# SyncE waits for the last scatter, and GpSimd has a second DRAIN

## The chip, the cores and the metric

The kernel runs on one NeuronCore of a Trainium2 chip (trn2). The metric is the time of one execution on the device in microseconds, lower is better. All data are float32, a few tables are bfloat16. The core has five engines with an instruction queue each: TensorE (PE in the profile, its weight loads PEld), VectorE (DVE), ScalarE (ACT), GpSimd (POOL) and SyncE (SP). A q behind a name (POOLq) is the engine's queue or sequencer. DMAs are issued from SP, ACT and POOL.

## The reference: what is computed

`x` has 4 x 256 tokens of 256 channels. Four residual steps follow each other:

```python
x = x + tanh(g_xattn[0]) * graph_attention(ctx_512, layernorm(x), ...)   # two layers
x = x + tanh(g_ffn[0])   * gated_ffn(layernorm(x), ...)                   # 704 wide
x = x + tanh(g_xattn[1]) * top_k_attention(ctx_512, layernorm(x), Wq, Wk, gamma)
x = x + tanh(g_ffn[1])   * mixture(layernorm(x), gate_w, w1, w2, w3)
```

The change touches the end of the last step, the mixture of experts. Eight experts of width 512 stand ready, and each token uses the two with the highest scores:

```python
h = silu(einsum('th,efh->etf', x, w1)) * einsum('th,efh->etf', x, w3)
y = einsum('etf,ehf->eth', h, w2)
coef = (one_hot(sel, 8) * mult[..., None]).sum(axis=1)
out = einsum('te,eth->th', coef, y)
```

## The kernel before, in words

Each engine has its own program, and semaphores order them. The normalised tokens are stored as rows in DRAM (`xn3_dram`), and `x` after the attention is stored in the output (`out`) by SP. The mixture then works in blocks of 128 tokens that share an expert. For each block POOL gathers the block's rows from `xn3_dram` with an indirect DMA, TensorE turns them and multiplies them by the expert's weights, ScalarE and VectorE do the activation and the product, TensorE multiplies by `w2`, ScalarE scales the result by the token's coefficient (`scale_y`), and POOL adds the rows to `out` with an indirect DMA that accumulates (a scatter).

There are 16 blocks with a place of their own (`STATIC` = 16). Blocks 0 to 7 are of the first half of the tokens, blocks 8 to 15 of the second. `AT` = 10: between block 9 and block 10 stands a loop over pairs of overflow blocks, whose number is read from data; on these inputs it runs once. An overflow block gathers with `fetch_over` and scatters in two halves of 64 rows (`scatter_over`).

Scatters are in strict order. `scatter(j)` waits on the semaphore `scattered` until every scatter before it has landed, since two blocks can add to the same row. After the last one, the program before waits once more at line 769 for all of them, and at line 771 for the gathers of the overflow blocks, which were issued long before. Then the program ends.

The end of the program is not written in the kernel: the instructions that close it are put down under line 69. Each engine has a branch, a DRAIN (an instruction that is finished when the engine has finished what is behind it), and then a meeting of all five engines by EVENT_SEMAPHORE instructions, which POOL gathers and releases. At the program's start (line 2262) stands such a meeting too, with a DRAIN on each engine.

POOL's order of work is a list, `POOL_ORDER`, that is written out by hand; the loop at lines 735 to 749 goes through it. Around the place of the change it reads: scatter 5, the gathers of overflow blocks 0 and 1 (line 715), scatter 6, gathers 10 and 11, scatter 7, gathers 12 and 13, scatter 8, the gathers of overflow blocks 2 and 3, scatter 9, gathers 14 and 15. Scatters of blocks are line 707, gathers of blocks line 687, and the gathers of the graph step (`gather_rows`) line 666.

SP's program issues loads and stores, and ends with waits for its stores (lines 582 and 583). It has nothing else to do from there on.

The semaphores `row_picked` tell VectorE that a gather of line 666 has landed; before there were eight of them, one for each tile.

Of the kernel before, what the change touches and what calls it, by code (L numbers as in the profile page):

```python
# [43 lines left out]
HT = T // 2  # L44
# [18 lines left out]
def build(nc, x_in, ctx2_in, g_xattn, g_ffn, gamma, w0_in, w0T_in, b0_in, w1_in, w1T_in, a_in, b1_in,  # L63
# [5 lines left out]
    with ctx:  # L69
# [3 lines left out]
        def sem(name):  # L73
            return ctx.enter_context(nc.semaphore(name))
# [256 lines left out]
        feat_exp = sem("feat_exp")  # L331
        token_ready = sem("token_ready")
        feat_stored = [sem(f"feat_stored{b}") for b in range(B)]
        row_picked = [sem(f"row_picked{t}") for t in range(T)]
        x_squared = sem("x_squared")
        norms_ready = sem("norms_ready")
        lead_ready = sem("lead_ready")
# [54 lines left out]
        y_done = sem("y_done")  # L392
        y_scaled = sem("y_scaled")
        scattered = sem("scattered")

        CONSTS = 23
        HIDDEN_BANK = FEAT_BANK = (6, 4)
# [67 lines left out]
                      ("gather", 0), ("gather", 1), ("gather", 2), ("gather", 3), ("attn_stats", 2), ("attn_stats", 3),  # L465
                      ("gather", 4), ("gather", 5), ("gather", 6), ("gather", 7), ("moe_stats", 2), ("moe_stats", 3),
                      ("scatter", 0), ("scatter", 1), ("scatter", 2), ("scatter", 3), ("gather", 8), ("scatter", 4), ("gather", 9),
                      ("scatter", 5), ("gather_over", 0), ("gather_over", 1), ("scatter", 6), ("gather", 10), ("gather", 11), ("scatter", 7),
                      ("gather", 12), ("gather", 13), ("scatter", 8), ("gather_over", 2), ("gather_over", 3), ("scatter", 9),
                      ("gather", 14), ("gather", 15)]  # L470

# [43 lines left out]
        @block.sync  # L515
        def _(sp):
            xv = x_in.rearrange("(t p) c -> p t c", p=P)
            sp.dma_start(ctx2[:, 0:N], ctx2_in[:, 0:N]).then_inc(ctx_loaded[0], 16)
            sp.dma_start(w0x[:, 0:H * FO], w0_in).then_inc(w0_loaded, 16)
            sp.dma_start(w1x[:, :, 0:H * FO], w1_in.rearrange("(k p) n -> p k n", p=P)).then_inc(w1_loaded, 16)  # L520
            sp.dma_start(x[:, 0:HT, :], xv[:, 0:HT, :]).then_inc(x_loaded[0], 16)
            sp.dma_start(ctx2[:, N:2 * N], ctx2_in[:, N:2 * N]).then_inc(ctx_loaded[1], 16)
            sp.dma_start(gates[:, 0:2], rows(g_xattn)).then_inc(gates_loaded, 16)
            sp.dma_start(gates[:, 2:4], rows(g_ffn)).then_inc(gates_loaded, 16)
            sp.dma_start(gates[:, 4:5], rows(gamma)).then_inc(gates_loaded, 16)
            sp.dma_start(x[:, HT:T, :], xv[:, HT:T, :]).then_inc(x_loaded[1], 16)
            def load_up(w, src):
                sp.dma_start(w[:, :, :], src.rearrange("(k p) n -> p k n", p=P)).then_inc(ffn_loaded, 16)

            load_up(gw, gw_in)  # L530
            def load_expert(e):
                load_weights(e, ((e1, e1_in), (e3, e3_in), (e2, e2_in)))

            def load_weights(e, pieces):
                for w, src in pieces:
                    sp.dma_start(w[:, e * 1024:(e + 1) * 1024], src[e]).then_inc(experts_loaded[e], 16)

            def load_down():
                sp.dma_start(dw[:, 0:FULL, :], dw_in[0:FULL * P, :].rearrange("(k p) n -> p k n", p=P))\
                  .then_inc(down_loaded, 16)  # L540
                sp.dma_start(dw[P - TAIL:P, FULL, :], dw_in[FULL * P:INTER, :]).then_inc(down_loaded, 16)
                sp.dma_start(dsr[:, :], rows(ds_in)).then_inc(down_loaded, 16)

            def load_general():
                sp.dma_start(b1[:, :], rows(b1_in)).then_inc(b1_loaded, 16)
                for q in range(2):
                    sp.dma_start(ctxT.rearrange("d (c q n) -> d c q n", c=2, q=2)[:, :, q, :],
                                 ctx2_in[q * D:(q + 1) * D, :].rearrange("d (c n) -> d c n", c=2)).then_inc(whole_ctx_loaded, 16)

            for b in range(B):  # L550
                if b == 2:
                    load_up(uw, uw_in)
                    for v, src in ((gs, gs_in), (us, us_in)):
                        sp.dma_start(v[:, :], src).then_inc(ffn_loaded, 16)
                    load_general()
                sp.wait_ge(token_ready, b + 1)
                sp.dma_start(f_dram[b].rearrange("(t p) c -> p t c", p=P),
                             feat[:, 2 * b:2 * b + 2, :]).then_inc(feat_stored[b], 16)
            load_down()
            sp.dma_start(rg[:, :, :], rg_in.rearrange("(k p) n -> p k n", p=P)).then_inc(router_loaded, 16)  # L560
            sp.wait_ge(graph_over, T)
            for e in (0, 1, 2, 3, 4, 7):
                load_expert(e)
            for p, (t, n) in enumerate(PARTS):
                if p == 2:

                    sp.wait_ge(ffn_u_done, 2 * FULL)
                    sp.wait_ge(ffn_g_done, 2 * IT)
                    for e in (5, 6):
                        load_weights(e, ((e1, e1_in), (e3, e3_in)))  # L570
                    sp.wait_ge(down_done, len(PARTS))
                    for e in (5, 6):
                        load_weights(e, ((e2, e2_in),))

                sp.wait_ge(x3_ready, p + 1)
                sp.dma_start(out.rearrange("(t p) c -> p t c", p=P)[:, t:t + n, :],
                             xr[:, t:t + n, :]).then_inc(out_stored[p], 16)
                sp.wait_ge(xn_ready, XT["turn_moe", p] + 1)
                sp.dma_start(xn3_dram.rearrange("(t p) c -> p t c", p=P)[:, t:t + n, :],
                             xn[:, t % HT:t % HT + n, :]).then_inc(rows_stored[p], 16)  # L580
            for p in range(len(PARTS)):
                sp.wait_ge(out_stored[p], 16)
                sp.wait_ge(rows_stored[p], 16)


        @block.gpsimd
        def _(pool):
# [72 lines left out]
            def gather_rows(b):  # L660

                pool.wait_ge(index_ready, b // 2 + 1)
                pool.wait_ge(feat_stored[b], 16)
                for t in range(2 * b, 2 * b + 2):
                    pool.sem_inc(pool_passed)
                    pool.indirect_dma_start(  # L666
                        out=picked[:, t, :], out_offset=None, in_=f_dram[b],
                        in_offset=bass.IndirectOffsetOnAxis(ap=gix[:, t:t + 1], axis=0),
                        bounds_check=last_node, oob_is_err=False).then_inc(row_picked[t], 16)

            def wait_rows(h):

# [19 lines left out]
            def scatter(j):  # L692

                h, at = place(j)
                if j == 0:
                    pool.wait_ge(out_stored[0], 16)
                    pool.wait_ge(out_stored[1], 16)
                if j == E:
                    pool.wait_ge(out_stored[2], 16)
                    pool.wait_ge(out_stored[3], 16)  # L700
                pool.wait_ge(y_scaled, j + 1)
                if j >= AT:
                    pool.wait_ge(scattered, pairs * 64 + 16 * j)
                elif j:
                    pool.wait_ge(scattered, 16 * j)
                pool.sem_inc(pool_passed)
                pool.indirect_dma_start(  # L707
                    out=out, out_offset=bass.IndirectOffsetOnAxis(ap=ids[h][:, at:at + 1], axis=0),
                    in_=yv[kept_in(j)], in_offset=None,
                    bounds_check=bound, oob_is_err=False, compute_op=ALU.add).then_inc(scattered, 16)  # L710

            def fetch_over(rows, q):

# [21 lines left out]
            for name, *at in POOL_ORDER:  # L735
                if (name, *at) in LN:
                    deviations(name, *at)
                elif name == "hidden_low":
                    hidden_low(*at)
                elif name == "spread":  # L740
                    spread(*at)
                elif name == "gather_rows":
                    gather_rows(*at)
                elif name == "gather":
                    gather(*at)
                elif name == "gather_over":
                    gather_over(*at)
                elif name == "scatter":
                    scatter(*at)

            pool.wait_ge(list_ready, 4)
            pairs = pairs_in_use(pool)
# [13 lines left out]
                    scatter_over(q, 1)  # L766
            for j in range(AT, STATIC):
                scatter(j)
            pool.wait_ge(scattered, pairs * 64 + 16 * STATIC)
            for q in range(2):  # L770
                pool.wait_ge(over_gathered[q], pairs * 16 + 32)

# [272 lines left out]
        def _(dve):  # L1045
# [264 lines left out]
            def add_graph(p):  # L1310
# [3 lines left out]
                for i in range(3):  # L1314
                    t = 2 * p + i
                    if i < 2:
                        dve.wait_ge(row_picked[t], 16)
                        dve.scalar_tensor_tensor(out=x[:, t, :], in0=picked[:, t, :], scalar=tg[:, 0:1], in1=x[:, t, :],  # L1318
                                                 op0=ALU.mult, op1=ALU.add).then_inc(graph_over, 1)
                    if i:  # L1320
# [948 lines left out]
```

## Time and profile before

| what | value |
|---|---|
| times of three runs | 222.89, 223.87, 224.24 us |
| median | 223.87 us |
| span of the profiled execution | 221.5 us |
| PE busy | 202.0 us (91%) |
| POOL busy | 87.0 us (39%) |
| last matmul ends | 208.4 us |
| last scatter is issued at | 212.97 us |
| POOL's closing DRAIN | from 217.1 us, 4.157 us long |

The profiled execution has no time of its own beside its span; the span of 221.5 us lies 2.4 us below the median of the three runs, and this is what lies around the program (the launch and its end). Start times are microseconds from the start of the span. In a row of an engine's timeline, "idle before" is how long the engine did nothing before that instruction, and the name behind the arrow is what ended the idle time. DRAIN and the other instructions of a queue are not counted as busy, so POOL's 87.0 us don't hold the 4.157.

### The profile page before, as it was taken

The numbers are of one execution on the slowest core, as the hardware profiler recorded it, in microseconds if no ns is written. First come the engines' busy times: TensorE is split into PE (matmuls) and PEld (weight loads), VectorE is DVE, ScalarE is ACT, GpSimd is POOL, SyncE is SP. The second block draws the span as 40 slices with busy tenths as digits, with TensorE's granted clock in tenths as the row PEclk, the third lists the DMA queues.
The fourth block names the chain that finished last, engine by engine and source line by source line (L and its number), as shares of the span: only waits on it lengthen the run. The fifth ranks groups of instructions, "written<-read, shape, count | busy, mean of one in ns | idle before, by whom it ended". The sixth has DMA issues, their size and how long they took to land.

```text
span 221.5 us, 3823 instructions
## 1 busy us (share of the span) xinstructions
PE 202.0 (91%) x1282; PEld 158.5 (72%) x1282; DVE 134.4 (61%) x461; ACT 85.5 (39%) x188; POOL 87.0 (39%) x107
## 2 busy tenths in 40 slices
PE   8999989999999989999989999999999999999600
PEld 7787754444875347779879989999953799999500
DVE  3698697999979969997886595925137311111100
ACT  2777653998002373034172172222245332222100
POOL 8256218320011110082813234466768547224320
PEclk9999999999999999999999999999999999999955
DMA  5848227149998145434340321322333010222130
GB/s 175 222 185 267 65 94 206 47 166 374 408 421 337 50 139 201 183 102 179 114 162 0 40 36 22 64 37 44 74 50 48 26 14 8 28 24 25 22 40 6
DMA packets 16795, 26.07 MB, mean 118 GB/s; under 512 B 4094, under 2 KB 12421, under 8 KB 16774
## 3 DMA queue, kind: packets, MB, share of 16 engines
q1 hardware_dynamic: 11328, 20.14, 25.3%
q0 software_dynamic: 4064, 5.25, 13.4%
q10 hardware_dynamic: 1382, 0.41, 1.1%
q8 instruction: 11, 0.18, 0.3%
q14 instruction: 10, 0.08, 0.1%
HBM read 21.34 MB, written 5.51 MB: 121 GB/s over the span
## 4 chain that ended last, share of the span: by engine, by line
PE 34%; DVE 32%; DMA 14%; issue 8%; ACT 7%; POOL 2%; DVEq 1%; POOLq 0%; ACTq 0%
PE PS L2077 12%; DMA out_dram<-a,ids_late 8%; PE PS L2109 6%; DMA out_dram<-zb,sidx 5%; PE PS L1780 3%; PE PS L2120 3%; DVE stat L1066 3%; DVE hT L1458 3%; ACT a L837 2%; PE PS L1844 2%; DVE work L1144 2%; DVE x L1318 1%; DVE mv L1073 1%; DVE work L1130 1%; DVE top L1140 1%
## 5 line engine op out<-in xcount | busy, mean ns | idle before, releaser
L2077 PE MATMUL PS<-hT,e 128*128 128x128 f32 x512 | 62.0, 276 | 1.1 <-ACT hT L966 1.1
L2077 PEld LDWEIGHTS PS<-hT,e 128*128 128x128 f32 x512 | 60.1, 192 | 2.9 <-ACT hT L966 1.9
L1962 PE MATMUL PS<-xnT,e 128*128 128x512 f32 x88 | 39.6, 598 | 1.9 <-DVE hT L1458 1.1
L1962 PEld LDWEIGHTS PS<-xnT,e 128*128 128x128 f32 x88 | 16.1, 190 | 22.1 <-issue 17.4
L1714 DVE TENSOR_TENSOR hT<-th,PS 128x512 f32<-128x512 f32 x15 | 10.3, 686 | 35.6 <-PE PS L2077 35.3
L2109 PE MATMUL PS<-e,hT 128*128 128x256 f32 x128 | 30.6, 382 | 0.2 <-DVE x L1496 0.2
L2109 PEld LDWEIGHTS PS<-e,hT 128*128 128x128 f32 x128 | 23.1, 190 | 2.8 <-issue 0.3
L644 POOL TENSOR_TENSOR rstd<-veps,nhalf 128x2 f32<-128x2 f32 x12 | 8.7, 727 | 39.4 <-DVE veps L1075 39.4
L707 POOL DMA_INDIRECT out_dram<-a,ids_early x8 | 13.4, 1676 | 23.2 <-ACT a L1000 13.2
L1976 PE MATMUL PS<-e,hT 128*128 128x256 f32 x96 | 21.7, 383 | 0.0
L1976 PEld LDWEIGHTS PS<-e,hT 128*128 128x128 f32 x96 | 17.9, 190 | 2.9 <-issue 0.5
L707 POOL DMA_INDIRECT out_dram<-a,ids_late x8 | 12.6, 1578 | 18.6 <-DMA out_dram<-a,ids_late 11.9
L976 ACT ACTIVATE th<-PS 128x512 f32<-128x512 f32 x16 | 9.5, 593 | 26.7 <-PE PS L2077 26.7
L687 POOL DMA_INDIRECT sim<-xn_rows,ids_early x8 | 8.6, 1080 | 19.8 <-DVE ids_early L1682 14.6
L666 POOL DMA_INDIRECT e<-graph_rows,gix x8 | 9.2, 1155 | 9.7 <-DMA graph_rows<-e 8.0
L934 ACT ACTIVATE x<-x,rs 128x256 f32<-128x256 f32 x8 | 4.4, 593 | 21.1 <-DVEq L1490 21.1
L1780 PE MATMUL PS<-ones 128*128 128x128 f32 x64 | 10.8, 326 | 1.0 <-POOL ones L596 1.0
L1000 ACT ACTIVATE a<-PS,coef_early 128x256 f32<-128x256 f32 x8 | 3.8, 473 | 19.3 <-PE PS L2109 16.2
L1780 PEld LDWEIGHTS PS<-ones 128*128 128x128 f32 x64 | 9.5, 230 | 1.4 <-POOL ones L596 1.0
L687 POOL DMA_INDIRECT sim<-xn_rows,ids_late x8 | 8.4, 1046 | 3.9 <-issue 2.1
L1458 DVE SCALAR_TENSOR_TENSOR hT<-th,us,PS 128x512 f32<-128x512 f32 (+1 forms) x12 | 9.0, 746 | 1.3 <-ACT th L927 1.2
L837 ACT ACTIVATE a<-sim,bar 128x256 f32<-128x256 f32 x16 | 7.9, 498 | 3.8 <-DVE bar L1105 3.8
(301 smaller groups left out, 318.6 us busy)
## 6 DMA issues: line engine op xcount, KB each, us to landing
e<-e_in SPq DMA_DIRECT2D x24, 512.0 KB, 8.7
x<-x_in SPq DMA_DIRECT2D x2, 512.0 KB, 6.0
graph_rows<-e SPq DMA_DIRECT2D x4, 256.0 KB, 2.2
out_dram<-x SPq DMA_DIRECT2D x4, 256.0 KB, 2.4
xn_rows<-xn SPq DMA_DIRECT2D x4, 256.0 KB, 2.4
e<-gw_in SPq DMA_DIRECT2D x1, 768.0 KB
e<-uw_in SPq DMA_DIRECT2D x1, 640.0 KB
e<-dw_in SPq DMA_DIRECT2D x1, 640.0 KB, 4.4
```

The source lines that it names most:

```text
L666: pool.indirect_dma_start(out=picked[:, t, :], out_offset=None, in_=f_dram[b], in_offset=bass.IndirectOffsetOnAxis(ap=gix[:, t:t + 1], axi ...
L687: pool.indirect_dma_start(out=xg[j % E], out_offset=None, in_=xn3_dram[0:(HN, B * N)[h], :], in_offset=bass.IndirectOffsetOnAxis(ap=ids[h] ...
L707: pool.indirect_dma_start(out=out, out_offset=bass.IndirectOffsetOnAxis(ap=ids[h][:, at:at + 1], axis=0), in_=yv[kept_in(j)], in_offset=No ...
L837: ins = act.activation(a2[:, t, :], sim[:, t, :], ACT.Sign, bias=bar[:, n, t:t + 1], accum_out=signs[:, t:t + 1])
L976: act.activation(th[:, j % 2, :], PS[:, j % 2, :], ACT.Silu).then_inc(silu_ready, 1)
L1458: dve.scalar_tensor_tensor(out=hT[at:P, it, :], in0=th[at:P, n % 2, :], scalar=us[at:P, it:it + 1], in1=PS[at:P, bank, :], op0=ALU.mult, o ...
L1714: dve.tensor_tensor(hh[me], th[:, me, :], PS[:, 2 + me, :], ALU.mult).then_inc(gated, 1)
L1780: pe.matmul(PS[:, bank, 0:P], ones[:, :], ones[:, :], start=True, stop=True)
L1962: mm = pe.matmul(PS[:, bank, :], w[:, k, it * P:(it + 1) * P], xnT[:, h, k, :], start=(k == 0), stop=(k == 1))
L1976: mm = pe.matmul(PS[:, 4 + a // 2, (a % 2) * 256:(a % 2 + 1) * 256], hT[:, it, a * P:(a + 1) * P], dw[:, it, :], start=(it == 0), stop=(it ...
L2077: mm = pe.matmul(PS[:, bank + q, f * P:(f + 1) * P], w[:, k * F + f * P:k * F + (f + 1) * P], xgT[x_at][:, k, :], start=(k == 0), stop=(k ...
L2109: mm = pe.matmul(PS[:, y_bank(j), q * C:(q + 1) * C], hh[q][:, f * P:(f + 1) * P], W2[expert_of(j)][:, f * C:(f + 1) * C], start=(f == 0), ...
```

## The change

There are three edits, and a fourth that makes room for one.

1. `("retire",)` is put into `POOL_ORDER` behind the gathers of overflow blocks 0 and 1 and ahead of scatter 6. It issues `pool.drain()`, a DRAIN on POOL in the middle of the program.
2. The last scatter (block 15) counts up a semaphore of its own, `last_scattered`, instead of `scattered`.
3. POOL's wait for all scatters at line 769 is gone, and SP waits for `last_scattered` at the end of its program.
4. `row_picked` has four semaphores instead of eight: tiles t and t + 4 share one, and VectorE waits for 16 with the first and 32 with the second.

```diff
-        row_picked = [sem(f"row_picked{t}") for t in range(T)]
+        row_picked = [sem(f"row_picked{i}") for i in range(HT)]
...
+        last_scattered = sem("last_scattered")
...
-                      ("scatter", 5), ("gather_over", 0), ("gather_over", 1), ("scatter", 6), ("gather", 10), ("gather", 11), ("scatter", 7),
+                      ("scatter", 5), ("gather_over", 0), ("gather_over", 1), ("retire",), ("scatter", 6), ("gather", 10), ("gather", 11), ("scatter", 7),
...
                 sp.wait_ge(out_stored[p], 16)
                 sp.wait_ge(rows_stored[p], 16)
+            sp.wait_ge(last_scattered, 16)
...
-                        bounds_check=last_node, oob_is_err=False).then_inc(row_picked[t], 16)
+                        bounds_check=last_node, oob_is_err=False).then_inc(row_picked[t % HT], 16)
...
-                    bounds_check=bound, oob_is_err=False, compute_op=ALU.add).then_inc(scattered, 16)
+                    bounds_check=bound, oob_is_err=False, compute_op=ALU.add)\
+                    .then_inc(last_scattered if j == STATIC - 1 else scattered, 16)
...
+                elif name == "retire":
+                    pool.drain()
...
-            pool.wait_ge(scattered, pairs * 64 + 16 * STATIC)
...
-                        dve.wait_ge(row_picked[t], 16)
+                        dve.wait_ge(row_picked[t % HT], 16 * (t // HT + 1))
```

No DMA and no work of an engine changes its place. What changes at the end is who waits. On POOL the end of the program read before (`a2` is the tile of the scaled rows, the register instruction works out the count for the wait, and the wait for `scattered` is row L771):

```order
L703 REGISTER_ALU [waits y_scaled]
L707 DMA out_0_dram<-a2,ids_late 1024x256 [waits scattered]
L703 REGISTER_ALU [waits y_scaled]
L707 DMA out_0_dram<-a2,ids_late 1024x256 [waits scattered]
L769 REGISTER_ALU
L771 ISA [waits scattered]
L69 UNCONDITIONAL_BRANCH [waits over_gathered1,over_gathered0]
```

and of the change:

```order
L705 REGISTER_ALU [waits y_scaled]
L709 DMA out_0_dram<-a2,ids_late 1024x256 [waits scattered]
L705 REGISTER_ALU [waits y_scaled]
L709 DMA out_0_dram<-a2,ids_late 1024x256 [waits scattered]
L775 ISA
L69 UNCONDITIONAL_BRANCH [waits over_gathered1,over_gathered0]
```

The last scatter's own issue still waits for the 15 scatters before it; behind it POOL waits for no scatter. These rows don't list DRAINs.

## Rows read from the trace of the kernel before

**Rows 1.** The page: TensorE, GpSimd and its granted clock in 40 slices of the span.
```profile
PE   8999989999999989999989999999999999999600
POOL 8256218320011110082813234466768547224320
PEclk9999999999999999999999999999999999999955
```

**Rows 2.** The chain of waits that ended last, its end: start us, us, what.
```profile
173.73 0.48 ACT zb L989
174.34 0.56 issue
175.13 3.21 DMA out_dram<-zb,sidx
...
203.98 3.77 DMA out_dram<-a,ids_late
207.79 0.76 issue
208.55 3.63 DMA out_dram<-a,ids_late
212.22 0.53 issue
212.97 1.56 POOL out_dram L707
```

**Rows 3.** Line 69, the closing: engine, instruction, count: min/median/max ns, first and last start us.
```profile
L69 POOLq EVENT_SEMAPHORE  x2: 17/17/17, 221.3 to 221.4; - x2
L69 SPq DRAIN  x1: 7/7/7, 116.8 to 116.8; - x1
L69 PEldq DRAIN  x1: 1312/1312/1312, 207.1 to 207.1; - x1
L69 POOLq DRAIN  x1: 4157/4157/4157, 217.1 to 217.1; - x1
```

**Rows 4.** Line 771, POOL's waits ahead of its closing, same columns.
```profile
L771 POOLq FUSED_REGOPS  x1: 37/37/37, 216.8 to 216.8; - x1
```

**Rows 5.** Line 2262, POOL's DRAIN at the start, ahead of all its DMAs.
```profile
L2262 POOLq DRAIN  x1: 173/173/173, 0.4 to 0.4; - x1
```

**Rows 6.** Groups of GpSimd's indirect DMAs: line, form, count | busy us, mean ns | idle before.
```profile
L707 POOL DMA_INDIRECT out_dram<-a,ids_early x8 | 13.4, 1676 | 23.2 <-ACT a L1000 13.2 <-DMA out_dram<-a,ids_early 7.1 <-PE PS L2063 2.9
L707 POOL DMA_INDIRECT out_dram<-a,ids_late x8 | 12.6, 1578 | 18.6 <-DMA out_dram<-a,ids_late 11.9 <-ACT a L1000 4.1 <-DMA out_dram<-zb,sidx 2.3
L666 POOL DMA_INDIRECT e<-graph_rows,gix x8 | 9.2, 1155 | 9.7 <-DMA graph_rows<-e 8.0 <-issue 1.7
L687 POOL DMA_INDIRECT sim<-xn_rows,ids_early x8 | 8.6, 1080 | 19.8 <-DVE ids_early L1682 14.6 <-DVE a L1212 3.3 <-issue 1.8
L687 POOL DMA_INDIRECT sim<-xn_rows,ids_late x8 | 8.4, 1046 | 3.9 <-issue 2.1 <-DVE over_ids L1686 1.7
L730 POOL DMA_INDIRECT out_dram<-zb,sidx x4 | 5.8, 1461 | 6.0 <-DMA out_dram<-zb,sidx 3.8 <-ACT zb L989 2.2
L715 POOL DMA_INDIRECT zc<-xn_rows,ids_late x4 | 4.3, 1079 | 1.2 <-issue 1.2
L715 POOL DMA_INDIRECT zc<-xn_rows,gidx x2 | 2.1, 1040 | 0.6 <-issue 0.6
```

**Rows 7.** GpSimd's timeline around the second DRAIN's place: start us, us, instruction [idle before].
```profile
147.85 1.02 POOL L715 DMA_INDIRECT zc<-xn_rows,ids_late  x1 [0.31 <-issue]
150.72 2.06 POOL L707 DMA_INDIRECT out_dram<-a,ids_early  x1 [1.85 <-ACT a L1000]
153.09 1.05 POOL L687 DMA_INDIRECT sim<-xn_rows,ids_late  x1 [0.30 <-issue]
...
156.52 1.60 POOL L707 DMA_INDIRECT out_dram<-a,ids_early  x1 [1.03 <-DMA out_dram<-a,ids_early]
...
161.86 1.62 POOL L707 DMA_INDIRECT out_dram<-a,ids_late  x1 [1.08 <-ACT a L1000]
163.78 1.19 POOL L715 DMA_INDIRECT zc<-xn_rows,ids_late  x1 [0.30 <-issue]
...
175.13 1.52 POOL L730 DMA_INDIRECT out_dram<-zb,sidx  x1 [2.19 <-ACT zb L989]
```

**Rows 8.** VectorE's timeline there.
```profile
150.00 1.30 DVE L1735 COPY x<-e 128x1024 f32 x2 [1.56 <-issue]
```

**Rows 9.** TensorE's timeline: the turns of gathered block 10 and overflow block 2.
```profile
162.16 0.38 PE L2063 MATMUL PS<-ident,sim 128*128 128x128 f32 x2
170.23 0.44 PE L2063 MATMUL PS<-ident,zc 128*128 128x128 f32 x2
```

**Rows 10.** DMAs from issue to landing: scatters (line 707), then overflow gathers (line 715).
```profile
DMA to landing us min/median/max: 3.6/3.8/5.0
```
```profile
DMA to landing us min/median/max: 2.2/2.3/2.7
```

## The prediction

> **What bounds the kernel now.** I read the page first. TensorE is busy in nearly every slice until the last three [rows 1], so for most of the program it is the bound. In the last slices it has nothing left, its granted clock has fallen to 0.5, and what little runs is on POOL. The chain of waits tells what that is [rows 2]: from 175.13 us on there is nothing in it but scatters, each from its issue to its landing, with about half a microsecond to 0.8 us of issue between them. The last one is issued at 212.97. The median scatter lands 3.8 us after its issue [rows 10], so this one lands near 212.97 + 3.8 = 216.77, and POOL's next instruction behind the wait starts at 216.8, which agrees [rows 4].
>
> The span ends at 221.5. What fills the 4.7 us from the landing on is not in the chain, since queue instructions aren't in it; the view of line 69 has it [rows 3]: POOL's DRAIN starts at 217.1 and lasts 4.157 us, to 221.26, and then comes the meeting of the engines, 0.25 us. SP has been at its own DRAIN, 7 ns, since 116.8 us, and waits there for the others. So the end of the program is serial: last landing, 0.33 us of queue, DRAIN, meeting.
>
> **What POOL's DRAIN pays for.** When it starts, POOL's last instruction (212.97 + 1.56 = 214.53) is 2.6 us past and the last DMA has landed. It waits for nothing that can be named and still takes 4.157 us. At the start of the program, with no DMA behind it, a DRAIN on POOL took 0.173 us [rows 5]. Between the two, POOL issued 8 + 8 + 8 + 8 + 8 + 4 + 4 + 2 = 50 indirect DMAs [rows 6]. My reading is that DRAIN goes through the DMAs that POOL has issued since the last DRAIN and closes the account of each. That gives (4.157 - 0.173) / 50 = 0.080 us for each. Two points don't prove a line; a fixed fee of 4.0 us as soon as there is any DMA fits them as well, and is a rival below.
>
> The Trainium skill says otherwise of a DRAIN (VectorE: DVE Perf Modes, section "The DRAIN you can't avoid"): those that are not VectorE's pipeline flush are boilerplate of about 12 ns, constant, on all five engines. By that the new DRAIN would be free, there would be no closing DRAIN to shorten, and the change would give nothing. SP's 7 ns agrees with it, POOL's 4157 ns contradicts it [rows 3].
>
> **The change, part by part.**
>
> *The wait moves from POOL to SP.* POOL issues the last scatter until 214.53 and then waits only for gathers that it issued before the last six scatters. Its DRAIN can begin with the 23 older DMAs at once, while the last scatter is still on its way for 216.77 - 214.53 = 2.2 us. SP wakes at the landing, and behind its wait stand only a branch and its 7 ns DRAIN; nothing else is queued there, and nobody but the meeting waits for SP. I give it 0.2 us.
>
> *The second DRAIN splits the account.* Ahead of its place POOL has issued 8 gathers of line 666, gathers 0 to 9, scatters 0 to 5 and 2 overflow gathers: 26. Behind it stand the other 24. If the fee is by DMA, the closing DRAIN has 0.173 + 24 x 0.080 = 2.09 us of work. All but the last DMA's share fits in the 2.2 us of the landing: it is through at about 214.53 + 2.09 = 216.6, waits for the landing at 216.77, and closes the last one, about 0.1 us. So POOL is ready at some 216.9 to 217.0, and SP too. With the meeting's 0.25 us and some queue time the span ends at about 217.25. Saved: 221.5 - 217.25 = 4.25 us.
>
> *What the second DRAIN costs where it stands.* POOL's gather ahead of it ends at 147.85 + 1.02 = 148.87 and lands at 147.85 + 2.3 = 150.15 [rows 7, 10]. DRAIN has 0.173 + 26 x 0.080 = 2.25 us of work and ends at 151.12, later than that landing. Scatter 6 then starts at 151.4 instead of 150.72, 0.7 us late. It may win some back: its issue took 2.06 us there, against 1.60 and 1.62 for the next two, while VectorE copied from 150.00 to 151.30 [rows 7, 8], and now it begins after that copy. Who waits for scatter 6? Scatter 7, which waited for its landing, and the gathers between. Scatter 8 had 1.08 us of idle before it, of which 0.30 is the usual gap, so 0.78 us of lateness is gone there. What is left meets the idle of 2.19 us before the first overflow scatter at 175.13, which waits for ScalarE and starts the serial chain; less the same gap that is 1.9. With the idle of 1.85 less 0.30 before scatter 6, the cover is 1.55 + 0.78 + 1.9 = 4.2 us for a DRAIN that needs 2.25. TensorE doesn't feel it: block 10's rows, issued at 153.09, are turned at 162.16, and overflow block 2's, issued at 163.78 and landed near 166.1, at 170.23 [rows 7, 9], 4 us later. ScalarE's waits for landed scatters ask for ones many blocks back. So I cost it at nothing; without that cover it would cost up to its 2.25 us. Bounds: 0.173 us (nothing by DMA), and, with the fixed fee and a wait for the landing first, 1.3 + 4.16 = 5.5 us, of which 1.3 would show.
>
> The Trainium skill speaks against this place (SBUF — State Buffer, the box "The DVE blocks DMA trap" under its two-sided view): while VectorE runs a float32 copy within SBUF, GpSimd is locked out of the shared port and can't write descriptors. The scatter's 2.06 us beside the copy agrees. If the DRAIN needs that port too, the copy's 1.30 us would come on top, 3.6 us in all, still under the cover of 4.2, and the sum stays.
>
> *Four semaphores fewer and one more, one wait and one register instruction less.* 37 ns on POOL, in parallel with the landing now. VectorE's waits for pairs on one semaphore end when they did before, as the later of the two is also the later to land. Nothing.
>
> **Sum.** 4.25 us off a span of 221.5. What lies around the span (2.4 us to the median) stays, so 223.87 - 4.25 = 219.6 us, 1.9% faster. The three runs before lie 1.35 us apart, and about 1% is what a measurement of this kernel can tell from no change.
>
> **The rivals.**
>
> *A fee that isn't split.* DRAIN costs 4.0 us however few DMAs there are, or the closing one goes through all 50 again: the second DRAIN then doesn't do what it is for. For it: only two points, 0.173 and 4.157. Against: a fixed fee of exactly that size has no other sign in the trace. The closing DRAIN starts at 214.53 and ends at 218.7, the span at 218.95. Saved 2.55, time 221.3. The second DRAIN would end at 148.87 + 4.16 = 153.0, within its cover. Chance 0.13.
>
> *The account is opened only at the landing.* DRAIN first waits for all transfers, then goes through them: 216.8 + 2.09 = 218.9, span 219.15, saved 2.35, time 221.5. The second DRAIN ends near 152.4, under cover. TensorE's DRAIN began at 207.1, while matmuls ran until 208.4, and ended with them [rows 3], so a DRAIN does begin before its engine is through. Chance 0.09.
>
> *Slower: both at once.* A fixed fee, paid after the landing. The second DRAIN ends at 150.15 + 4.16 = 154.3, 1.3 us beyond its cover, and the whole serial chain of scatters from 175.13 starts 1.3 us later. The closing DRAIN starts at 216.8 instead of 217.1 and gains 0.3. Time 223.87 + 1.0 = 224.9. It decides from a DRAIN of over 4.2 us at 148.87; to lose over 1% it would have to last about 6.7. Chance 0.04.
>
> *Nothing, within 1%.* The wait on SP takes up what POOL saves, or there is a queue time that I don't see, or DRAIN costs nothing to anybody, as the 12 ns rule has it: 223.9. Chance 0.04.
>
> **How the numbers follow.** My forecast has 0.70. Its own range is 219.0 to 220.3, from the three runs' scatter and the unsure 0.3 us at the end. The range for 8 in 10 takes in the two partly-gaining rivals at 221.3 and 221.5: 218.8 to 221.6. Faster by over 1% is below 221.63: all of the forecast, and more than half of the two rivals, which lie at its edge: 0.83. Within 1%: their rest and the last rivals, 0.14. Slower: 0.03.
>
> **What would show it.** In the profile of the changed kernel the closing DRAIN on POOL starts before 215 and ends with the last landing, within 0.3 us, however its length is counted. A second DRAIN of about 2.2 us stands near 149, and scatter 6 starts at about 151.4; scatter 8 and the first overflow scatter start when they did (161.86, 175.13). The last scatter is still issued near 213, and the span ends near 217.2. If the second DRAIN is 4 us long, the fee is fixed; if it's about 3.6, the port matters; if the closing one ends at about 218.7 to 219, a rival holds. My prediction is wrong if the scatter chain starts later than before, or the time of the closing doesn't follow the number of DMAs.

## The result and the profile after

The changed kernel takes 220.37 us (median of 5 runs, 220.25 to 220.97) against 223.9 before (median of 5, of which one, 227.04, was in a slower state and is not in the ratio). The ratio is 0.986, with a 95% interval of 0.984 to 0.988: 1.4% faster, and the interval doesn't reach no change. On two other occasions it was 0.985 (0.983 to 0.987) and 0.983 (0.980 to 0.986). The forecast was 219.6. The measured time is just above the forecast's own range, which ended at 220.3, and inside the range for 8 in 10, 218.8 to 221.6.

The gain is where it was looked for. First the view of line 69 of the changed kernel, the closing instructions (engine, instruction, count, ns, first and last start in us), which answers to [rows 3], and under it SP's new wait, which answers to [rows 4]:

```profile
L69 POOLq EVENT_SEMAPHORE  x2: 17/17/17, 218.7 to 218.8; - x2
L69 POOLq DRAIN  x1: 4666/4666/4666, 214.0 to 214.0; - x1
L69 SPq DRAIN  x1: 7/7/7, 217.9 to 217.9; - x1
```
```profile
L585 SPq EVENT_SEMAPHORE  x1: 28/28/28, 217.6 to 217.6; - x1
```

POOL's DRAIN now starts while the last scatter is still being issued. Its record holds the rest of that issue and the flight of the scatter, so its length doesn't measure its work. What counts is its end, 214.0 + 4.67 = 218.67. SP is through its wait at 217.6, which dates the landing, and is ready at 217.9. These rows give the start to one decimal only. The trace itself is finer: the last update of the scatter's semaphore, which is the landing here and below, is at 217.62, and the DRAIN ends at 218.65. So POOL is the last, 1.03 us behind the landing, and that is what the forecast did not have.

GpSimd's timeline of the changed kernel (start us, us, instruction, idle before), which answers to [rows 7], with its last row:

```profile
145.47 1.56 POOL L709 DMA_INDIRECT out_dram<-a,ids_early  x1 [2.58 <-ACT a L1004]
147.34 1.06 POOL L718 DMA_INDIRECT zc<-xn_rows,ids_late  x1 [0.30 <-issue]
148.71 1.02 POOL L718 DMA_INDIRECT zc<-xn_rows,ids_late  x1 [0.31 <-issue]
153.21 1.61 POOL L709 DMA_INDIRECT out_dram<-a,ids_early  x1 [3.47 <-PE PS L2067]
...
157.95 1.60 POOL L709 DMA_INDIRECT out_dram<-a,ids_early  x1 [0.31 <-issue]
...
162.72 1.62 POOL L709 DMA_INDIRECT out_dram<-a,ids_late  x1 [0.52 <-issue]
...
175.99 1.52 POOL L733 DMA_INDIRECT out_dram<-zb,sidx  x1 [2.79 <-ACT zb L993]
...
213.89 1.56 POOL L709 DMA_INDIRECT out_dram<-a,ids_late  x1 [3.01 <-DMA out_dram<-a,ids_late]
```
```profile
L754 POOLq DRAIN  x1: 5907/5907/5907, 146.4 to 146.4; - x1
```
```profile
150.85 1.29 DVE L1739 COPY x<-e 128x1024 f32 x2 [1.55 <-issue]
```

The reader has to find the second DRAIN in a hole: it isn't counted as busy, so scatter 6 (the row at 153.21) shows 3.47 us of idle, put down to a TensorE instruction. The queue's row of line 754 tells the truth: the DRAIN's record starts at 146.4 and ends at 152.3, 2.6 us behind the gather's issue, which ended at 149.73. From there 0.9 us more pass until scatter 6 starts.

In this execution the last scatter is issued at 213.89, 0.92 us later than in the profiled execution of before. That isn't the second DRAIN: scatter 5, ahead of it, is already 0.86 late (145.47 against 144.61). From scatter 5 to the first overflow scatter it is 175.99 - 145.47 = 30.52 us, and before it was 175.13 - 144.61 = 30.52 too. The number to compare is therefore the time from the start of the last scatter to the end of the span: 221.5 - 212.97 = 8.5 us before, 218.9 - 213.89 = 5.0 us now. Gained: 3.5 us, of 4.25 forecast.

### The profile page after: what moved, and what is told of

The parts are those of the page before. It is cut to its first block, busy times and chain, and to the rows that moved or that the text cites. A ratio compares the mean times of both kernels' runs of the same rounds, so it can differ in the third digit from the quotient of the medians.

```text
span 218.9 us, 3823 instructions
## 1 busy us (share of the span) xinstructions
PE 202.9 (93%) x1282; PEld 158.8 (73%) x1282; DVE 134.5 (61%) x461; ACT 85.6 (39%) x188; POOL 85.8 (39%) x107
## 4 chain that ended last, share of the span: by engine, by line
PE 35%; DVE 29%; DMA 14%; issue 9%; ACT 7%; POOL 3%; DVEq 1%; POOLq 0%; ACTq 0%
PE PS L2081 13%; DMA out_dram<-a,ids_late 9%; PE PS L2113 6%; DMA out_dram<-zb,sidx 4%; PE PS L1784 3%; PE PS L2124 3%; DVE stat L1070 3%; DVE hT L1462 3%; ACT a L841 2%; PE PS L1848 2%; DVE work L1148 2%; DVE x L1322 1%; DVE mv L1077 1%; PE PS L1835 1%; DVE work L1134 1%
## 5 line engine op out<-in xcount | busy, mean ns | idle before, releaser
L709 POOL DMA_INDIRECT out_dram<-a,ids_early x8 | 12.9, 1607 | 24.4 <-ACT a L1004 11.4
```

Source lines behind the costliest of these rows:

```text
L709: pool.indirect_dma_start(out=out, out_offset=bass.IndirectOffsetOnAxis(ap=ids[h][:, at:at + 1], axis=0), in_=yv[kept_in(j)], in_offset=No ...
```

## The experiments

The theories. **A** is that of the prediction: a DRAIN on POOL costs 0.08 us for each DMA since the last DRAIN, and all but the last one's share runs beside the flying transfer. **B**: 0.064 us for each beside the transfer, and a fixed 0.95 us once both this and the landing are past. **C**: the fee isn't split by the second DRAIN. **D**: a part that grows with the number of DMAs comes after the landing. B and D were formed on the profile after.

**One half alone: only SP's wait.**

```diff
-                      ("scatter", 5), ("gather_over", 0), ("gather_over", 1), ("retire",), ("scatter", 6), ...
+                      ("scatter", 5), ("gather_over", 0), ("gather_over", 1), ("scatter", 6), ...
```

> The second DRAIN is taken out; SyncE still waits for the last scatter. The closing DRAIN has all 50 DMAs before it. Theory A (0.080 us for each DMA and 0.17 fixed, gone through from the end of the last issue on): it ends 4.2 us after the last scatter's issue ends, so the span from that scatter's start to the program's end is 1.56 + 4.2 + 0.25 = 6.0 us, against 8.5 before and 5.0 with the change. Theory B (0.064 us for each DMA beside the flying transfer, and a fixed 0.95 us that comes after both this and the last landing): 50 x 0.064 + 0.95 = 4.15 us, the same 6.0. Rival C (the second DRAIN takes nothing off the closing one, all gain is from the wait): 5.0 us as with the change. Time: 221.4 by A and B, 220.4 by C.

Measured: 221.21 us beside 223.38 for before, ratio 0.989 (0.986 to 0.992). The last scatter of its profiled execution starts at 214.03 and the span ends at 220.1, 6.1 us later, as A and B had it. Line 69 and SP's wait:

```profile
L69 POOLq DRAIN  x1: 5767/5767/5767, 214.1 to 214.1; - x1
```
```profile
L585 SPq EVENT_SEMAPHORE  x1: 28/28/28, 217.8 to 217.8; - x1
```

DRAIN ends at 219.87, 4.28 us after the issue's end at 215.59, and 2.1 us after the landing. C falls. A and B both had it end some 4.2 us after the issue's end, so this run doesn't part them: with 50 DMAs either has work left when the scatter lands. Beside the change's 1.03 us with 24 DMAs it gives the first two points of what comes behind the landing.

**The other half alone: only the second DRAIN.**

```diff
             for j in range(AT, STATIC):
                 scatter(j)
+            pool.wait_ge(last_scattered, 16)
```

> The second DRAIN stays, and GpSimd waits for the last scatter again ahead of its closing DRAIN, which then has 24 DMAs that have all landed. Theory A: DRAIN lasts 0.17 + 24 x 0.080 = 2.1 us. Theory B: 0.95 + 24 x 0.064 = 2.5 us. Rival C: 4.16 us as before. From the last scatter's start to the program's end: 6.5 by A, 6.9 by B, 8.5 by C; times 221.9, 222.2 and 223.9.

Measured: 221.23 us, ratio 0.990 (0.988 to 0.993). From the last scatter (212.33) to the end (218.7) 6.4 us. Its closing DRAIN:

```profile
L69 POOLq DRAIN  x1: 2031/2031/2031, 216.4 to 216.4; - x1
```

With 24 landed DMAs it lasts 2.03 us, against 4.16 with 50 [rows 3]: 0.082 us for each of the 26 that the second DRAIN took. A's 2.1 is right for landed DMAs, B's 2.5 is not. So each half of the change is worth about 1% alone, 2.1 to 2.4 us by the closing, and both together 3.5 us, less than the sum: with fewer DMAs there is less for SP's wait to hide.

**DRAINs in the quiet tail.**

```diff
             for j in range(AT, STATIC):
                 scatter(j)
+                if j in (12, 13):
+                    pool.drain()
+            pool.wait_ge(last_scattered, 16)
```

> DRAINs in the quiet tail, where VectorE and TensorE barely run: behind the scatter of block 12 (21 DMAs since the last DRAIN, this scatter in flight), behind that of block 13 (1 DMA, in flight), and the closing one with 2 DMAs, after a wait for the last scatter, all landed. Theory A: the first two end within 0.1 to 0.2 us of the landing, the closing one lasts 0.17 + 2 x 0.08 = 0.33 us. Theory B: the first two end 1.0 us after the landing, and the closing one lasts 0.95 + 0.13 = 1.1 us. Theory D (the part after the landing grows with the number of DMAs): the first ends about 0.9 us after the landing, the second 0.1, the closing one lasts 0.3.

One run, 221.02 us. The two DRAINs (line 775), then the closing one, then the scatters of blocks 12, 13 and 14 around them:

```profile
L775 POOLq DRAIN  x2: 4134/4318/4503, 199.7 to 204.9; - x2
```
```profile
L69 POOLq DRAIN  x1: 210/210/210, 218.6 to 218.6; - x1
```
```profile
199.62 1.55 POOL L709 DMA_INDIRECT out_dram<-a,ids_late  x1 [3.05 <-DMA out_dram<-a,ids_late]
205.16 1.56 POOL L709 DMA_INDIRECT out_dram<-a,ids_late  x1 [3.99 <-issue]
209.96 1.55 POOL L709 DMA_INDIRECT out_dram<-a,ids_late  x1 [3.24 <-ACT a L1007]
```

The first (21 DMAs) took 4.503 us and ends at 204.25. Its scatter landed at 203.34: 0.91 us behind. The second (1 DMA) took 4.134 and ends at 209.08, the landing is at 209.00: 0.08. The closing one (2 DMAs, landed) lasts 0.21. B wanted 1.0, 1.0 and 1.1, A 0.1 to 0.2 twice and 0.33. D alone is near in all three (0.9, 0.1 and 0.3). It also shows the price of a DRAIN in the serial chain: 205.16 - 199.62 = 5.54 us to the next scatter, where 4.6 is usual.

**Fewer DMAs in the closing DRAIN.**

```diff
-                      ... ("gather_over", 1), ("retire",), ("scatter", 6), ("gather", 10), ("gather", 11), ("scatter", 7),
+                      ... ("gather_over", 1), ("gather", 14), ("scatter", 6), ("gather", 10), ("gather", 11), ("gather", 15), ("scatter", 7),
...
-                      ... ("scatter", 9), ("gather", 14), ("gather", 15)]
+                      ... ("scatter", 9), ("retire",)]
```

> The second DRAIN stands behind scatter 9, just ahead of the overflow loop, and gathers 14 and 15 go where GpSimd was idle (ahead of scatters 6 and 7), so 38 DMAs are ahead of it and 12 behind. Theory D, made precise by the runs before (DRAIN goes through its DMAs twice, 0.041 us each time and DMA: once at once, once after the last landing; fixed 0.05): the second DRAIN ends 0.1 + 38 x 0.041 = 1.7 us after scatter 9 lands, before GpSimd is wanted for the overflow scatters; the closing one ends 0.1 + 12 x 0.041 = 0.6 us after the last landing, against 1.0 with the change. From the last scatter's start to the end: 4.6 us; time 0.4 us less than the change. Theory B (a fixed 1 us after the landing): 5.0 us and the change's time. Theory A: 4.1 us.

Measured: 219.28 us, ratio 0.982 (0.979 to 0.985). The last scatter starts at 212.39, the span ends at 216.9: 4.5 us, where D had 4.6, B 5.0 and A 4.1. The second DRAIN (line 753) ends at 171.74, 1.60 us after scatter 9 landed (170.14). The first overflow scatter isn't held up by it: it starts at 174.85, 30.52 us behind scatter 5, as before. The closing DRAIN ends at 216.66, 0.54 us after the landing (216.12; SP's wait is line 584):

```profile
L753 POOLq DRAIN  x1: 5658/5658/5658, 166.1 to 166.1; - x1
```
```profile
L69 POOLq DRAIN  x1: 4172/4172/4172, 212.5 to 212.5; - x1
```
```profile
L584 SPq EVENT_SEMAPHORE  x1: 28/28/28, 216.1 to 216.1; - x1
```

**More DMAs in it.**

```diff
-                      ("gather", 4), ("gather", 5), ("gather", 6), ("gather", 7), ("moe_stats", 2), ("moe_stats", 3),
+                      ("gather", 4), ("gather", 5), ("gather", 6), ("gather", 7), ("moe_stats", 2), ("moe_stats", 3), ("retire",),
...
-                      ... ("gather_over", 1), ("retire",), ("scatter", 6), ...
+                      ... ("gather_over", 1), ("scatter", 6), ...
```

> The second DRAIN stands ahead of scatter 0 instead, where GpSimd is idle for 8 us: 16 DMAs ahead of it, 34 behind. Theory D: the closing DRAIN ends 0.1 + 34 x 0.041 = 1.5 us after the last landing, 3.65 us after the last issue ends, and 5.4 us pass from the last scatter's start to the end. Theory B: 5.0 us. Theory A: 0.17 + 34 x 0.08 = 2.9 us after the issue ends, 4.7 us in all. Time by D 0.4 us more than the change.

Measured: 220.49 us, ratio 0.987 (0.984 to 0.990). From the last scatter (212.61) to the end (218.1) 5.5 us: D's 5.4, not B's 5.0 nor A's 4.7. The second DRAIN, now of 16 DMAs, ends 1.39 us after GpSimd's instruction ahead of it. The closing one ends at 217.8, SP's wait at 216.4:

```profile
L69 POOLq DRAIN  x1: 5101/5101/5101, 212.7 to 212.7; - x1
```
```profile
L585 SPq EVENT_SEMAPHORE  x1: 28/28/28, 216.4 to 216.4; - x1
```

**DRAINs beside VectorE.** The change, and three DRAINs more.

```diff
-                      ("gather_rows", 3), ("norm_var", 2), ("norm_var", 3),
+                      ("gather_rows", 3), ("norm_var", 2), ("norm_var", 3), ("retire",), ("retire",),
...
-                      ... ("moe_stats", 2), ("moe_stats", 3),
+                      ... ("moe_stats", 2), ("moe_stats", 3), ("retire",),
```

> Three more DRAINs in places where GpSimd is idle and VectorE busy: two behind the variance of the last attention block (8 DMAs, then 0, all landed long ago) and one ahead of scatter 0 (8 DMAs). Theory D, if VectorE's work does not get in its way: the first lasts 0.05 + 8 x 0.082 = 0.70 us, the second 0.05. The rule on the shared port, if it holds for DRAIN: longer, by up to the length of a copy. The DRAIN at its place has 10 DMAs instead of 26 and ends about 0.5 us after the last landing instead of 1.3, so scatter 6 starts 0.8 us earlier against its neighbours. The closing one is as with the change. Time as with the change.

One run, 220.41 us. The view of the drains' line in three stretches of time (the first row is the first DRAIN, the second covers the first and the second one, the third is the one ahead of scatter 0), and POOL's instructions ahead of the first and the third:

```profile
L754 POOLq DRAIN  x1: 1472/1472/1472, 47.7 to 47.7; - x1
L754 POOLq DRAIN  x2: 41/756/1472, 47.7 to 49.2; - x2
L754 POOLq DRAIN  x1: 1464/1464/1464, 111.6 to 111.6; - x1
```
```profile
47.77 0.69 POOL L646 TENSOR_TENSOR rstd<-veps,nhalf 128x2 f32<-128x2 f32 x1 [1.88 <-DVE veps L1079]
111.65 0.69 POOL L646 TENSOR_TENSOR rstd<-veps,nhalf 128x2 f32<-128x2 f32 x1 [0.35 <-DVE veps L1079]
```

POOL's engine is through at 48.46 and 112.34; the DRAINs of 8 DMAs end at 49.2 and 113.1, 0.7 us later as expected, and the one of none lasts 0.041 us. VectorE was busy beside them and nothing was added. At the old place, with 10 DMAs instead of 26, scatter 6 has 2.82 us of idle before it instead of 3.47. That DRAIN and VectorE's copy beside it say more about the shared port:

```profile
L754 POOLq DRAIN  x1: 5252/5252/5252, 146.0 to 146.0; - x1
```
```profile
150.43 1.29 DVE L1739 COPY x<-e 128x1024 f32 x2 [1.55 <-issue]
```

The gather ahead of it lands at 150.80, when the copy is already running, and the DRAIN ends at 151.25, 0.45 us later, while the copy still runs to 151.72. So the copy doesn't hold up what a DRAIN does behind the landing.

**The semaphores alone.** The kernel before, with four `row_picked` semaphores.

```diff
-        row_picked = [sem(f"row_picked{t}") for t in range(T)]
+        row_picked = [sem(f"row_picked{i}") for i in range(HT)]
```

> The kernel before with the four shared row_picked semaphores and nothing else of the change. All theories: no difference, 223.4 us, 8.5 us from the last scatter's start to the end.

Measured: 223.72 us beside 223.44, ratio 1.000 (0.998 to 1.002); 213.67 to 222.2 is 8.5 us. Nothing, as expected.

**The change again, twice, and the later DRAIN again.**

> The change itself, unaltered, on the same chip as the runs beside it. All theories: 220.4 us, the closing DRAIN ends 1.0 us after the last landing, 5.0 us from the last scatter's start to the program's end.

> The change, unaltered, beside the next kernel on the same chip. All theories: 220.2 us, about 5.0 us from the last scatter's start to the program's end.

> The kernel with the second DRAIN behind scatter 9, once more, beside the change. Theory D: 12 instead of 24 DMAs in the closing DRAIN, 12 x 0.041 = 0.5 us less than the run beside it, 4.5 us from the last scatter's start to the end. Theory B: the same as the change.

The change took 220.0 and 219.92 us, ratios 0.985 (0.983 to 0.987) and 0.983 (0.980 to 0.986), with 5.1 us from the last scatter to the end both times (215.93 to 221.0 and 213.18 to 218.3). The later DRAIN took 220.04 us this time, ratio 0.983 (0.981 to 0.986), with 4.6 us (213.42 to 218.0). So the 0.5 us at the end are there again, but the two kernels run side by side can't be told apart in time. In this profiled execution it lost 1.0 us elsewhere: VectorE's copy of overflow weights ahead of overflow block 0's product starts at 164.83, in the first execution of the same kernel at 163.88, scatter 5 standing at 144.33 in both:

```profile
164.83 0.74 DVE L1738 COPY wbuf<-e 128x1024 f32 x1 [4.74 <-issue]
```
```profile
163.88 0.69 DVE L1738 COPY wbuf<-e 128x1024 f32 x1 [4.58 <-issue]
```

The second DRAIN, which ends at 171.65, comes after that. Why the copy starts late in some executions was not tried. No version is shown to beat the change.

## Why the prediction was right, and where it was not

All DRAINs of POOL together. First with everything landed: how long it takes for n DMAs; then with the last DMA in flight: how long after its landing the DRAIN ends, by the trace's own times. 10, 26 and 38 are DRAINs in the middle, the others stand at the end or in the tail; 12 and 24 were seen in two and four executions, 26 in five and 38 in two, all within 0.02 us.

| n, landed | 0 | 2 | 24 | 50 |
|---|---|---|---|---|
| us | 0.04 | 0.21 | 2.03 | 4.16 |

| n, last in flight | 1 | 10 | 12 | 21 | 24 | 26 | 34 | 38 | 50 |
|---|---|---|---|---|---|---|---|---|---|
| us after the landing | 0.08 | 0.45 | 0.54 | 0.91 | 1.03 | 1.10 | 1.45 | 1.60 | 2.10 |

The first row is 0.045 + 0.082 n, within 0.02; the second 0.04 + 0.041 n, within 0.02. So half of the fee for all n DMAs waits for the last landing, and the other half is done before. It goes by the DMA and not by the rows that it moves: four of the last 24 move 64 rows instead of 128, and the 24 cost 0.083 us each, the 26 before them 0.082. Two passes over the DMAs, the second held up by the last one, would give just that. No run looks inside a DRAIN, so that there are two passes is an inference; that half of the fee comes after the landing is measured, at eight sizes besides n = 1.

*The bound at the end.* Right: POOL's DRAIN was the serial end of the program, and SP is ready 0.3 us after the landing.

*A fee by the DMA.* Right, against 0.13 for a fee that isn't split: the 0.080 us read from two points is 0.082, and the split takes 2.1 us off the closing DRAIN. The rule of 12 ns for a boilerplate DRAIN (the Trainium skill, VectorE: DVE Perf Modes, "The DRAIN you can't avoid") holds here for SP (7 ns), and neither for POOL nor for TensorE (1312 ns, with matmuls still running [rows 3]).

*"All but the last DMA's share fits in the 2.2 us of the landing".* This is the step that failed. The size of the sum was right (2.09 us forecast, 2.03 measured with all landed), its place wasn't: only half runs beside the transfer, 1.03 us comes behind it instead of 0.1. The prediction's own sign, a closing DRAIN that ends within 0.3 us of the last landing, failed with it. The rival that opened the account at the landing put all of it there and was as wrong on the other side. That the time came out between the forecast and these rivals, 3.5 us gained between 2.35 and 4.25, is this half.

*The cost of the second DRAIN.* Hidden, as forecast, but scatter 6 is 1.6 us late against scatter 5 (7.74 us after it, 6.11 before), not 0.7. Two terms were too small. The DRAIN ends 2.6 us behind the gather, not 2.25: the gather landed at 151.22, and the half of the fee that comes behind the landing, 0.04 + 26 x 0.041 = 1.1 us, puts the end at 152.3, later than both halves in a row would be (151.9). And from the DRAIN's end to scatter 6's start it is 0.9 us, as behind both DRAINs in the tail, where the forecast took the 0.3 us that lies between issues in a row. Scatter 7 is 0.6 us late, scatter 8 not at all (17.25 us in both). So the cover was enough for this; that it is 4.2 us was not tested, as no run had a longer DRAIN there.

*The port.* Scatter 6's issue fell from 2.06 to 1.61 us, as forecast: it no longer runs beside VectorE's copy. The Trainium skill's rule on the shared port (SBUF — State Buffer, "The DVE blocks DMA trap") has that scatter on its side. The DRAIN isn't held in the same way: with 26 DMAs what it does behind the landing ran beside the copy (150.85 to 152.14) and took 1.10 us, on the line of the table. Its end is 0.18 us behind the copy's, so this DRAIN alone could also be read as one that waits for the copy. The one with 10 DMAs can't: it ended 0.47 us before the copy did. The 3.6 us that the rule would have made of it did not come. What a DRAIN does before the landing was, by the table's sizes, over about when the copy began, so for that part the question stays open.

*The semaphores.* Nothing, as forecast.

*What lies around the span.* The 2.4 us that the forecast kept compares the span of one execution with the median of others. Where one execution has both numbers it is 2.0 to 2.1 us (220.97 and 218.9 for the changed kernel). The forecast is a difference, so this changes nothing in its 4.25 us.

## What to carry to other kernels

In this kernel a DRAIN on GpSimd settles all indirect DMAs since the last one, and the one at the program's end is on the path. In another kernel that issues such DMAs, look for it in the queue's rows, since neither the busy time nor the chain shows it. Let another engine wait for the last transfer, so that GpSimd reaches its DRAIN while the transfer flies, and put another DRAIN where GpSimd has idle time to spare, late enough that few DMAs are left. What stays behind the landing here is 0.04 us for each of those. A DRAIN whose place has no idle time costs its time: in the serial tail it made 4.6 us from one scatter to the next into 5.5.

## What the runs showed of the hardware that was not expected

That a DRAIN with a transfer in flight does half its work before the landing and half after: 2.1 us behind it with 50 DMAs, 0.08 with one. That it made little difference whether the DMAs are gathers alone (8 in 0.7 us) or scatters alone (2 in 0.21). That a float32 copy on VectorE, beside which a scatter's issue took 2.06 us instead of 1.61, added nothing to what a DRAIN does behind the landing. And that a DRAIN in the middle, at 26 DMAs, cost the program nothing although scatter 6 was 1.6 us late.
